# Register loads of tile numbers that begin on multiples of 16 bytes, in a fused graph and feed-forward kernel

## What is computed

```
x = x + gnn0(norm(x))    # mean over neighbours: segment_sum(x[nbr], dst) / count, then two products
x = x + ffn0(norm(x))    # 8 experts, top 2
x = x + gnn1(norm(x))    # attention over the edges, 8 heads
x = x + ffn1(norm(x))    # 16 experts, top 2, then a last norm

# gnn1, per edge: h = x W;  diff = h[dst] - h[src]
lin = hs.a1 + hd.a2 + diff.a3 + |diff|.a4 + (hs*hd).a5
att = softmax of leaky_relu(lin) over the edges of one src
out = segment_sum(att * h[dst], src)
```

## Time and profile before

| what | us |
|---|---|
| median of 3 runs | 2803.92 |
| lowest and highest of them | 2797.9 and 2806.47 |
| the profiled execution | 2802.34 |
| its span, first to last instruction | 2800.6 |
| first sum, about | 384 to 950 of the span |
| scores, about | 1523 to 2121 |
| second sum, about | 2160 to 2405 |

### The profile page before, as it was taken

One profiled execution on the slowest core, in us unless ns is written; L12 is line 12 of the kernel. 1 busy time (PEld: TensorE's weight loads), 2 busy tenths in 40 slices (PEclk: granted clock), 3 DMA queues, 4 the chain that ended last, 5 costly groups with the idle time before them and its releaser, 6 DMA issues. The chain is left out here.

```text
span 2800.6 us, 62667 instructions
## 1 busy us (share of the span) xinstructions
PE 2169.2 (77%) x15064; PEld 1758.9 (63%) x15065; DVE 1641.8 (59%) x4125; ACT 1452.4 (52%) x3570; POOL 1399.7 (50%) x1434
## 2 busy tenths in 40 slices
PE   4888866676777769999946888888884989759990
PEld 3655543344444559999934778778773777549990
DVE  8889853333333553333356777777777778853337
ACT  6778853333333243343437766666664888422335
POOL 0000037777777323333313777777770999325540
PEclk9999986666665679999967999999995999879995
DMA  3310025633333521111133777877782988632224
GB/s 110 104 44 17 18 82 177 194 104 105 104 104 103 106 86 34 37 37 35 34 114 96 234 235 229 231 230 226 224 219 48 287 268 260 227 140 69 71 66 143
DMA packets 182437, 367.93 MB, mean 131 GB/s; under 512 B 30426, under 2 KB 67716, under 8 KB 182126
## 3 DMA queue, kind: packets, MB, share of 16 engines
q1 hardware_dynamic: 118489, 208.65, 22.0%
q0 software_dynamic: 53760, 148.67, 20.6%
q10 hardware_dynamic: 10133, 9.97, 1.1%
HBM read 275.35 MB, written 91.83 MB: 131 GB/s over the span
## 5 line engine op out<-in xcount | busy, mean ns | idle before, releaser
L938 PE MATMUL sum_ps<-weightsL_w 128*128 128x256 f32 x880 | 379.6, 580 | 177.9 <-DMA weightsL_w<-y_gnn,sum_index 105.7
L853 POOL DMA_INDIRECT scores_rows<-h_gnn,scores_index x440 | 426.3, 969 | 146.2 <-issue 123.5
L853 POOL DMA_INDIRECT weightsL_w<-y_gnn,sum_index x440 | 418.2, 950 | 132.8 <-issue 129.1
L938 PEld LDWEIGHTS sum_ps<-weightsL_w 128*128 128x128 f32 x880 | 226.5, 284 | 330.7 <-issue 298.3
L953 DVE TENSOR_TENSOR sums_acc<-sums_acc,sum_ps 128x256 f32 x440 | 185.1, 421 | 365.6 <-PE sum_ps L938 294.5
L1578 ACT ACTIVATE sums_acc<-expertsL_hid_ps,expertsL_b 128x128 f32<-128x128 f32 x704 | 198.2, 373 | 303.0 <-PE expertsL_hid_ps L1527 302.7
L1527 PE MATMUL expertsL_hid_ps<-sums_acc,expertsL_w 128*128 128x128 f32 x2816 | 337.3, 277 | 4.6 <-DVE sums_acc L1598 2.8
L1527 PEld LDWEIGHTS expertsL_hid_ps<-sums_acc,expertsL_w 128*128 128x128 f32 x2816 | 327.1, 193 | 5.1 <-issue 5.0
L1539 PE MATMUL expertsL_out_ps<-weightsL_w,sums_acc 128*128 x1408 | 323.6, 379 | 0.0
L1502 POOL DMA_INDIRECT ys_L<-sums_acc,ffnL_result x120 | 145.2, 1210 | 353.5 <-DVE sums_acc L1608 338.2
L913 ACT ACTIVATE weightsL_w<-all_count_f,all_slot_src 128x128 f32<-128x128 f32 x440 | 133.2, 387 | 343.9 <-PEq L942 333.6
(11 more groups left out here) (434 smaller groups left out, 4223.5 us busy)
## 6 DMA issues: line engine op xcount, KB each, us to landing
saved_gnn<-scores_rows SPq DMA_DIRECT2D x220, 264.0 KB
sum_rows<-saved_gnn SPq DMA_DIRECT2D x220, 264.0 KB, 3.2
weightsL_w<-in_L_ffn_W SPq DMA_DIRECT2D x16, 1024.0 KB, 8.8
weightsL_w<-in_L_ffn_w SPq DMA_DIRECT2D x32, 512.0 KB, 9.4
scores_lanes<-slot_lanes SPq DMA_DIRECT2D x44, 320.0 KB
sort_low_b<-low_lanes SPq DMA_DIRECT2D x32, 416.0 KB, 3.6
weightsL_w<-ys_L SPq DMA_DIRECT2D x6, 1280.0 KB, 12.5
weightsL_w<-y_gnn,sum_index POOLq DMA_INDIRECT x440, 2.8
```

The costliest lines, as they stand in the source:

```text
L853: pool.indirect_dma_start(out=self.rows[s] if isinstance(self.rows, list) else self.rows[:, s, :], out_offset=None, in_=table[:, :], in_of ...
L938: last = nc.tensor.matmul(ps[s % banks][:, 0:D], pick[h][:, s % HALF, :], g.rows[s], start=True, stop=True)
```

## The change

`tiles_of` takes the first element instead of a number of a part. In the first sum VectorE's loop runs over 22 turns and loads twenty numbers at the start of each. In the scores the load for the second half of the same turn (f = 0) begins two elements earlier, at 20i + 8, and loads twelve, of which the first two are not used; the one for the next turn's first half (f = 1) loads ten from 20(i + 1), as before. In the second sum the arguments are written otherwise and give the same elements.

```diff
--- before.py
+++ after.py
@@ -23,6 +23,7 @@
 SLOTS = 2 * HALF
 LENT = 16
 PAIRS = SLOTS // 2
+ALIGNED = 4
 Q = -(-Q // (2 * SLOTS)) * 2 * SLOTS
 QP = -(-Q // 16) * 16
 NOWHERE = QP * P
@@ -860,9 +861,9 @@
             gather(turn, turn % 2, turn == turns - 1)
 
 
-def tiles_of(nc, engine, e, part, count):
-
-    return nc.values_load_multi_w_load_instructions(e["tiles"][0:1, bass.ds(part * count, count)], engines=[engine], min_val=0, max_val=NT - 1,
+def tiles_of(nc, engine, e, first, count):
+
+    return nc.values_load_multi_w_load_instructions(e["tiles"][0:1, bass.ds(first, count)], engines=[engine], min_val=0, max_val=NT - 1,
                                                     skip_runtime_bounds_check_because="tiles are held under NT when the table is made")[1]
 
 
@@ -977,10 +978,10 @@
                 ve.drain()
                 nc.vector.reciprocal(e["per"][:, :], e["per"][:, :])
                 ve.drain()
-                with ve.Fori(0, 2 * turns) as i:
-                    tiles = tiles_of(nc, nc.vector.engine, e, i, HALF)
-                    for s in range(0, HALF, 2):
-                        add_pair(HALF * i + s, s, tiles[s:s + 2])
+                with ve.Fori(0, turns) as i:
+                    tiles = tiles_of(nc, nc.vector.engine, e, SLOTS * i, SLOTS)
+                    for s in range(0, SLOTS, 2):
+                        add_pair(SLOTS * i + s, s, tiles[s:s + 2])
                 ve.wait_ge(added, banks + Q)
 
 
@@ -1097,12 +1098,12 @@
                 for f in range(4):
                     choose(0, f)
                 with ve.Fori(0, turns - 1) as i:
-                    tiles = tiles_of(nc, nc.vector.engine, e, i, SLOTS)
+                    tiles = tiles_of(nc, nc.vector.engine, e, SLOTS * i, SLOTS)
                     for s in range(0, SLOTS, 2):
                         add_pair(SLOTS * i + s, s, tiles[s:s + 2])
                         if s % FOUR >= MINE - 1:
                             choose(i + 1, s // FOUR)
-                tiles = tiles_of(nc, nc.vector.engine, e, turns - 1, SLOTS)
+                tiles = tiles_of(nc, nc.vector.engine, e, SLOTS * (turns - 1), SLOTS)
                 for s in range(0, SLOTS, 2):
                     add_pair(SLOTS * (turns - 1) + s, s, tiles[s:s + 2])
                 ve.wait_ge(added, banks + Q)
@@ -2196,7 +2197,10 @@
                                 keep(2 * i + f - 1, other)
                             if more:
                                 choose(nxt, other)
-                                tiles = tiles_of(nc, nc.vector.engine, e, 2 * i + f + 1, HALF)
+                                if f == 0:
+                                    tiles = tiles_of(nc, nc.vector.engine, e, SLOTS * i + HALF // ALIGNED * ALIGNED, HALF + HALF % ALIGNED)[HALF % ALIGNED:]
+                                else:
+                                    tiles = tiles_of(nc, nc.vector.engine, e, SLOTS * (i + 1), HALF)
                         if more:
                             for q in ahead.get(p, ()):
                                 stage(nxt, other * HP + q, tiles)
```

## The result

The kernel before took 2805.19 us in the median of four runs (2797.9 to 2811.66), the changed one 2781.14 us (2778.36 to 2781.67). The ratio is 0.9913, with a 95% interval from 0.9887 to 0.9939: 24 us less, where 16 were forecast. The profiled execution of the changed kernel took 2778.36 us, its span is 2776.6 us.

A forecast was written before the change was run, and what follows sets the result against it. VectorE was taken to bound the scores by about 1.0 us a turn, GpSimd right under it. Scores -16 us, all else 0, took the 2803.92 us median to 2788; own range 2784 to 2794, 8 in 10 2782 to 2804.

The forecast's parts named there:

- Second sum: Second sum's loads: same addresses and counts as before, only written otherwise, so 0 us.
- The scores: Scores: VectorE's shorter load relieves 1.3 us a turn, the bound moves to GpSimd, and 16 us come off.
- joint wait: Sign in the scores: TensorE's wait for VectorE's joint product falls from 79.8 us to about 50.
- freed rows: Sign in the scores: GpSimd's wait for freed rows, 18.7 us over the stage, falls under 4 us.
- the tail: Scores after the last gather: moves with the gathers and keeps its length, 0 us, ends -2 and +1.
- The load of twelve: Scores, first half of a turn: twelve from 80i + 32 bytes taken at 1.0 us, where ten took 2.28.
- The model of four aligned numbers at once: VectorE's loads: four aligned words per fetch, the rest singly, 0.27 us each; twelve are three fetches, 0.81 us.
- the row of ten: Profile row for VectorE's loads of ten from a multiple of 80 bytes: 1.07 us.
- First sum: First sum: VectorE gains 2.0 us a turn, 44 us in 22, worth 0 under GpSimd's pace; ends -1 and +1.
- A: Scores: lateness comes from ScalarE's freeing copies, not VectorE's stall; some 5 us gained, 2799 us; chance 0.20.
- C: Scores: load of twelve priced by register, 0.228 us each, 2.74 us; 10 us slower, 2814 us; chance 0.08.
- B: Scores: turns reach the first sum's pace, 21.5 us gained, 2782 us; chance 0.08.

The follow-up runs named there:

- the drained kernel: The kernel before with 35 drains of VectorE added ahead of the first sum's loop and no load touched: ratio 1.0008 [0.998, 1.0036].
- the repeat with added loads: The changed kernel with extra register loads from aligned starts added ahead of the first sum's loop: scores 583.9 us, second sum 244.4 us.

## Why the prediction was right and where it failed

**The step that failed** is the sum over the stages outside the scores. The forecast took 16 us off the scores and held all else at zero, with ends of 1 or 2 us, and that part gave 7.6 us more. Two terms of it can be named. *"Second sum. The same addresses and counts as before, written otherwise: 0"* looked at the loads and not at the code around them: it lost 2.4 us because a longer loop body ahead of it moved its branch, shown by the drained kernel. And the last experts gave 2.5 us, one of two values that the stage takes from run to run with the same code, of which the profile of before had shown the longer one; here nothing shows an effect of the change. The remaining 2.7 us are spread over the first sum (-1.3; its end was -1), routes, experts, sort, join and softmax, each no more than a stage differs between two runs of the same kernel (the changed kernel's first sum 692.5 and 694.2 us, the experts with the scores' part alone 455.8 and 457.1). The low end of the range for 8 in 10, 2782 us, gave all of this together 6 us, as if the rest of the kernel could only repeat itself to the microsecond; the kernel came out at 2781.14. The upper end, 2804, had 16 us of room.

**The scores: mechanism and size right.** VectorE was the bound, by 26.22 - 25.55 = 0.7 us a turn (forecast about 1.0, against the pace of the first sum); relieved, the stage goes to the gathers' pace. Forecast -16 us, measured -16.4 here; the repeat with added loads gives 583.9, -13.8 against the one trace of before at this pace. Index copies 25.55 us apart (forecast 25.4), joint wait 45.4 us (forecast about 50), freed rows 3.7 us over the stage (under 4), all as the last part of the prediction asks. That the sum came out at 16.4 is in part luck, since it is split otherwise than I had it: the turns gave 14.2 us of the 16, and the tail 2.3 us, outside its bound of 2. I had argued that the tail keeps its length since its one long wait is for rows; waits for rows did stay (1.58 us before, 1.46 and 1.59 now). In the repeat with added loads the turns gave 13.2 us and the tail 0.7, so the forecast for the tail may well hold, and the turns are worth 2 to 3 us less than forecast.

**The load of twelve: taken at 1.0 us, costs 0.85 alone.** The model of four aligned numbers at once gave 0.81 and was the right one; I had pulled it towards the row of ten, which is dearer for its two single numbers. In the stage it is dearer: the 22 loads of twelve take 0.85 to 1.53 us, 1.12 in the mean. But the 22 old loads that they replace took 2.62 us in the mean, not 2.28, so the relief on them was 1.5 us a turn where I had 1.3; the loads of ten of the other half went from 1.21 to 1.30 us, which leaves 1.4 us. What lengthens the loads in the scores is not shown. As the gathers' pace was the stop, the difference does not show in the time.

**First sum: right.** 22 loads of 1.35 us instead of 44, 44 us of VectorE's time saved, and turns of 25.16 instead of 25.20 us. The part alone came out at 1.0006 and 1.0017, both with 1 inside the interval.

**The rivals.** A (only the name changes) is out: GpSimd's waits went, and with them the time. C (slower, each number at 0.228 us) is out by the row of 0.85 us. Its price is right for starts off 16 bytes: twelve from there take 2.72 us, where it said 2.74. The Trainium skill, Runtime: NRT & Kernel Launch, section Instruction fetch mechanics, with its 200 ns a register, agrees with those 0.22 us and not with aligned loads, where a number comes to 0.07 us in twenties. The table loaded here lies in SBUF, a case of which the section says nothing. B (2782) is nearest by its number, but that is chance, for its mechanism did not happen: the turns did not come to the first sum's 25.16 us, and the gathers still take 968 ns.

**What stays open.** Why the clock rises at once or late in the last experts. Why twelve to twenty numbers from a fixed address, of which only the last is used, take 0.70 us and not 0.85 to 1.35. Why TensorE takes up gathered rows so late on some chips in the first sum, and what makes the scores longer there. Why the tail was shorter in the first pair. And the parts alone were never timed on a chip like the first, so the split of the 24 us is read there from stages, not from medians.

## What to carry to other kernels

A group of numbers loaded into VectorE's registers should start on a multiple of 16 bytes and have a multiple of four of them, even where some are read for nothing: twelve cost 0.85 us, ten 1.07, and ten off the multiple 2.28. It is worth time only where that engine sets the pace, so judge it by stage, and find the next bound first, for it caps the gain (here 0.7 us of 1.4 a turn). And a forecast's range must take in what untouched stages do from run to run and when their code moves: 2 to 3 us each here, as much as many changes are worth.

## What was not expected of the hardware

- The same loop branch on VectorE costs 190 or 289 ns by where its code lies, 2.1 us in 21 turns. In the experts' loops the same move changed the branch between 190 and 320 ns without any effect on the time, as VectorE is not late there.
- The same program needs 2800 us on some chips and 3171 to 3187 on others. In the one trace of it from there, all of the difference lies in the stages whose rows are gathered: a turn of twenty gathers goes from 25.2 to 30.8 us in the first sum, and from 26.2 to 37.5 in the scores.
- One short stage behind the second sum, 74 us in nearly all runs, took 87 us in three of them, with different kernels and on three chips. This was seen and not followed.
